# Graph network stack on one core: ScalarE writes the first sum's table rows and first parts from the output banks

## What is computed

```python
def _sage_layer(h, src, dst, W_l, b_l, W_r):
    msgs = h[src]
    agg = segment_sum(msgs, dst, N)
    cnt = segment_sum(ones, dst, N)
    return (agg / maximum(cnt, 1)) @ W_l + b_l + h @ W_r
h = relu(_sage_layer(x, src, dst, W1_l, b1, W1_r))
```

## Time and profile before

| | |
|---|---|
| median of 3 runs | 8222.67 us |
| the profiled execution, own time | 8213.33 us |
| its span | 8211.5 us |
| granted TensorE clock, mean of the span | 0.642 |
| stretch from the end of the last edge convolution's carries to the first sum's first matmul | 6478 to 6571 us |
| first sum, 49 blocks | 6571 to 6870 us |

### The profile page before, as it was taken

The page is one execution under the profiler, slowest core; times in us unless marked ns, Lnnn a source line. Parts: engine busy times, 40 slices in busy tenths (PEclk is TensorE's granted clock), DMA queues, the critical chain, the costliest instruction groups (busy, mean ns, idle before and its releaser), DMA issues.

```text
span 8211.5 us, 69615 instructions
## 1 busy us (share of the span) xinstructions
PE 4235.5 (52%) x19184; PEld 2465.7 (30%) x19184; DVE 5538.0 (67%) x13229; ACT 1494.4 (18%) x2140; POOL 4891.3 (60%) x5030
## 2 busy tenths in 40 slices
PE   2100000000155655656555555556565498999999
PEld 1000000000131111111113111111111298999999
DVE  4765555555578888888886888888888775222222
ACT  0222222222231121111111111111211200010000
POOL 6777777777637777777776777777777600000000
PEclk6555555555566565565655555565555599999999
DMA  5333333333224444444443444444444275766767
GB/s 145 86 93 86 85 86 85 86 85 86 66 86 130 129 129 132 131 130 130 129 130 103 129 130 132 130 130 129 130 131 131 80 263 201 267 225 227 268 220 247
DMA packets 642303, 1132.83 MB, mean 138 GB/s; under 512 B 164860, under 2 KB 422287, under 8 KB 641634
## 3 DMA queue, kind: packets, MB, share of 16 engines
q1 hardware_dynamic: 360256, 440.38, 16.7%
q0 software_dynamic: 159184, 251.10, 15.5%
q10 hardware_dynamic: 122578, 438.40, 13.4%
HBM read 716.67 MB, written 412.70 MB: 138 GB/s over the span
## 4 chain that ended last, share of the span: by engine, by line
POOL 57%; PE 20%; issue 18%; DVE 3%; ACT 1%; DMA 1%; DVEq 0%; POOLq 0%; ACTq 0%; SPq 0%
POOL CG L449 55%; PE psB L723 6%; PE psX L723 6%; PE psA L723 6%; PE psO L668 1%; POOL ad_starts L461 1%; POOL EG L506 1%; ACT X L1001 1%; POOL EG L441 0%; PE psX L660 0%; PE psO L783 0%; DVE BUF L1120 0%; DVE EG L1172 0%; PE psO L671 0%; DVE halves L1176 0%
## 5 line engine op out<-in xcount | busy, mean ns | idle before, releaser
L449 POOL DMA_INDIRECT CG<-table,BUF x4704 | 4532.5, 964 | 1564.2 <-issue 1432.1
L695 PE MATMUL psO<-WE,BUF 128*128 128x384 f32 x1568 | 1137.3, 880 | 106.8 <-DMA BUF<-in_edge_attr 99.8
L766 PE MATMUL psA<-ident,F 128*100 128x128 f32 x1 | 0.5, 452 | 1740.0 <-DVEq L1404 1740.0
L475 POOL CAST CG<-EG x35 | 26.9, 769 | 1297.9 <-DVEq L1173 1297.9
L953 ACT COPY psX<-BUF 128x384 f32<-128x384 f32 x392 | 189.0, 482 | 3210.7 <-DVE STG L1531 1618.2
L695 PEld LDWEIGHTS psO<-WE,BUF 128*128 128x128 f32 x1568 | 460.6, 324 | 619.4 <-DMA BUF<-in_edge_attr 371.6
L1429 DVE TENSOR_TENSOR terms<-CG,ARENA 128x32 f32<-128x32 f32 x196 | 45.1, 230 | 792.5 <-DMA CG<-table,BUF 792.0
L1493 DVE TENSOR_SCALAR BUF<-iota,EG 128x392 bf16<-128x392 f16 x1568 | 542.3, 346 | 0.0
L766 PEld LDWEIGHTS psA<-ident,F 128*100 128x100 f32 x1 | 0.2, 158 | 1740.3 <-DVEq L1404 1740.3
L702 PE MATMUL psB<-BUF 128*128 128x392 bf16 x523 | 251.2, 480 | 511.4 <-DVE BUF L1499 511.2
L702 PE MATMUL psA<-BUF 128*128 128x392 bf16 x523 | 252.1, 482 | 506.4 <-DVE BUF L1499 506.4
(11 more groups left out here) (279 smaller groups left out, 7912.3 us busy)
## 6 DMA issues: line engine op xcount, KB each, us to landing
BUF<-counts SPq DMA_DIRECT2D x245, 784.0 KB, 5.8
BUF<-counts ACTq DMA_DIRECT2D x245, 784.0 KB, 6.2
counts<-BUF SPq DMA_DIRECT2D x1572, 98.0 KB, 2.4
hist<-CG ACTq DMA_DIRECT2D x392, 384.0 KB, 2.5
hist<-CG ACTq DMA_DIRECT2D x196, 416.0 KB, 2.6
CG<-table,BUF POOLq DMA_INDIRECT x4704
BUF<-in_edge_attr SPq DMA_DIRECT2D x392, 128.0 KB
table<-TB SPq DMA_DIRECT2D x14, 336.0 KB, 2.6
```

What stands on the lines that cost most here:

```text
L449: pool.indirect_dma_start(out=rows_in[:, u % RING, k, :], out_offset=None, in_=tab, in_offset=bass.IndirectOffsetOnAxis(ap=SRC[:, u * S + ...
L695: mm = pe.matmul(ETERM[:, s, a, 0:4 * DIM], EA[:, s, a, :], WE[:, m, :, :].rearrange("k c d -> k (c d)"), start=True, stop=True)
```

## The change

For the first averaging layer alone (`f == MEAN1`), `root_rows` on ScalarE now waits for the output banks itself and makes three copies of each group: table rows to the bf16 first part, table rows to `TBW`, root rows to `R`. `take_rows` on VectorE waits for the first two and only subtracts. The other layers are as before.

```diff
@@ build: semaphores
+    first_made = sem("first_made")
@@ def root_rows(f, g):
+            if f == MEAN1:
+                here = slice(g * GB, (g + 1) * GB)
+                act.wait_ge(out_ready, out_group_base(f, "rows") + g + 1)
+                nc.scalar.copy(PARTS[:, here, 0:DIM], OUTG[:, :, 0:DIM]).then_inc(first_made, 1)
+                nc.scalar.copy(TBW[:, here, :], OUTG[:, :, 0:DIM]).then_inc(table_made, 1)
+                nc.scalar.copy(R[:, here, :], OUTG[:, :, DIM:2 * DIM]).then_inc(out_used, 1)
+                return
             act.wait_ge(table_made, PASS_OF_PHASE[f] * NG + g + 1)
             nc.scalar.copy(R[:, g * GB:(g + 1) * GB, :], OUTG[:, :, DIM:2 * DIM]).then_inc(out_used, 1)
@@ def take_rows(f, g):
             here = slice(g * GB, (g + 1) * GB)
+            if f == MEAN1:
+                dve.wait_ge(first_made, g + 1)
+                dve.wait_ge(table_made, PASS_OF_PHASE[f] * NG + g + 1)
+                link(tt(EGW[:, here, :], TBW[:, here, :], PARTS[:, here, 0:DIM], ALU.subtract))
+                dve.sem_inc(rest_made, 1)
+                return
             dve.wait_ge(out_ready, g + (out_group_base(f, "rows") + 1))
```

## The result

| | before | after |
|---|---|---|
| median of 22 runs, same chips | 8221.73 us (8218.61 to 8228.09) | 8234.67 us (8229.73 to 8238.70) |
| ratio, 95% interval | | 1.0015 (1.0009 to 1.0020) |
| profiled execution, own time / span | 8213.33 / 8211.5 us | 8235.68 / 8233.9 us |
| stretch: fill of XTQ's bias row to the first matmul of the first sum | 93.1 us | 105.3 us |
| from there to the end | 1640.3 us | 1635.6 us |

The change makes the kernel 12.9 us slower, 0.15%. The spans of the two profiles differ by 22.4 us, but 15 of these lie ahead of the stretch (it starts at 6478.1 us in one, at 6493.0 in the other), in gather passes that the change does not touch. Their length differs from execution to execution: in the nine profiles of this document that come from chips of like speed, the stretch starts anywhere from 6476.7 to 6493.0 us.

What follows compares the result with a forecast made beforehand. Gathering on GpSimd bounds most of the kernel; in the changed 93 us stretch, VectorE's chain does. 0.9 + 8.5 + 1.05 + 1.1 = +11.6 us on the median 8222.67 gives 8234 us, range 8226 to 8243.

Steps and rivals of the forecast that it cites:

- ScalarE's order as the deciding thing: In ScalarE's program the new copies stand behind its wait for scales_known, so VectorE must wait for them mid-chain.
- Group 0: First group's subtraction on VectorE, starting at 6506.67 instead of 6505.74 behind ScalarE's copies: +0.9 us.
- Groups 1 to 3: Middle periods: VectorE's subtraction waits for ScalarE's copies, each period 2.8 us longer instead of 1.78 shorter; +8.5 us.
- The copy to bf16: ScalarE's first-part copy from PSUM: taken to cost 0.71 us like the fp32 copy, with 1.57 as the upper end.
- Rival B: First-part copy on ScalarE costs 1.57 us instead of 0.71, seven times in the path: +17.6, 8240.3 us; chance 0.10.
- Collisions with GpSimd: VectorE's large operations, shifted by 3.8 us, meet GpSimd's parts for groups 0 and 1: +1.1 us, from 0 to 1.1.
- Tail: End of the stretch, last groups' root-row copies, multiplies and the count-block load: three links, +1.05 us together.
- The two links over the bank copies: In the tail, root-row copies queue third on ScalarE, delaying the multiplies of groups 5 and 6: +0.36 and +0.34 us.
- The load's +0.35: In the tail, ScalarE's count-block load is queued behind the last root-row copy, delaying TensorE's first sum: +0.35 us.
- the low end: If ScalarE's sequencer runs ahead of its copies, the count-block load could go out about 1 us earlier.
- TensorE's clock: Granted clock in the tail's two multiplies: taken as 0, with ends of +1.3 and -3.2 us.
- After the stretch: Everything behind the first sum's start was to take as long as before: no change.

## Why the prediction was right

Forecast 8234 us, measured 8234.67; forecast +11.6 us, measured +12.9 (and +9.8 on another chip). The mechanism and its main terms, group 0 and groups 1 to 3, are right. That the total agrees to 1 us is luck: in the tail, a load term with the wrong sign was made up for by a slower clock, and the 3.2 us that came back after the stretch by a remainder that no profile explains. Step by step:

- **ScalarE's order as the deciding thing**: shown by the run that moves only the copies (stretch 92.9) and by the one that adds one (5.44 for 4.83).
- **Group 0**, +0.9: the subtraction came 1.0 us later, relative to the start of the stretch.
- **Groups 1 to 3**, +8.5: 2.9 us each, 8.7. The idle time is 4.83 (4.6 forecast), the period of a group 14.7 (14.6 forecast).
- **The copy to bf16**, taken at 0.71 between 0.71 and 1.57: 0.71. Rival B's price did not appear.
- **Collisions with GpSimd**, +1.1: in the period of group 1, VectorE lost 0.29 + 1.02 + 0.42 + 1.13 = 2.9 us instead of 2.0, so +0.9. In the profile from the chip that gathers slowly the collisions fall into other periods and make +1.1.
- **Tail**, +1.05: measured +1.6 in the first pair of profiles, of other parts. The two links over the bank copies were +0.35 each, as reckoned. The load's +0.35 was wrong: ScalarE's sequencer issues it ahead of its own queued copies, 0.70 us after the multiply instead of 1.56. That was named as the low end and is the case; it gives 0.7 back, so without the clock the tail is at nothing and not at +1.05. TensorE's clock, taken at nothing, gave +0.9 and +0.65 in this pair of profiles, more than the upper end of +1.3 that the prediction took from the 4.69 us, and less in others (the tail's last multiply: 4.82, 3.84, 4.82 in the three profiles of the changed kernel).
- **After the stretch**, nothing was forecast: 3.2 us came back in the next layer's node phase. So "All that comes after the first sum's start should take as long as before" was wrong, the largest miss of the prediction.

Stretch and rest together make +8.3 us over the mean of the profiles (11.5 - 3.2); the medians say +12.9 (7.4 to 16.4) and +9.8 (2.5 to 18). The remainder of 1.5 to 4.6 us lies within these intervals. Whether part of it is in the gather passes ahead of the stretch was not resolved, as their length varies by more than that between executions.

## What to carry to other kernels

Moving work to an idle engine helps only if that engine's program reaches it before the user of the result asks for it. Read the user's timeline for the moment at which it asks, and the idle engine's for the place that the work gets in its order and for what that place waits for. An engine busy for a third of a stretch can be the latest all the same. Here one and the same offload cost 12 us, cost nothing, or went with a gain of 18 (8 of them to be had without it), by where the copies stood in ScalarE's program and where the subtractions stood in VectorE's; when an offload disappoints, try to move the consumer later before giving it up.

## What was not expected of the hardware

- ScalarE's sequencer runs ahead of its engine: the load was issued at 6593.52, 0.05 us after the start of the second of three copies that stand ahead of it in the program. Before, a wait for VectorE's copy stood ahead of it and held it back.
- The granted TensorE clock in one phase went with a difference of about 1 us in TensorE's idle time some 300 us earlier (5.3 to 5.5 us against 6.2 to 6.5): 44.2 to 44.4 us against 47.2 to 47.5 in thirteen profiles, without an exception. Only one of them, with the load held back, changed nothing else.
